# x and the value weights transposed on the host, a second head projected before the first step, a feed-forward loop written out

## The reference

```python
q, k, v = x @ wq, x @ wk, x @ wv              # 8 heads of 128
q, k = rope(q), rope(k)
p = softmax(q @ k.T / 128, causal)
x = layernorm(x + sum over heads of (p @ v) @ wo)
xn, se = rms_norm(x) * gamma_x, rms_norm(slots) * gamma_slot
logits = xn @ se.T                            # 512 slots
slots_in = softmax over the 8 experts (logits).T @ xn
proc = gelu(slots_in @ w1) @ w2
x = layernorm(x + softmax over the 512 slots (logits) @ proc)
```

## Time and profile before

| What | us |
|---|---|
| median of 3 runs | 1684.44 |
| lowest, highest | 1684.43, 1685.83 |
| the profiled execution's own time | 1682.29 |
| its span, first to last instruction | 1680.5 |

### The profile page before, as it was taken

How to read it: one execution, slowest core, us unless ns; L and a number is a source line. 1 busy time by engine, 2 the same in 40 slices (tenths; PEclk the granted TensorE clock), 3 DMA queues, 4 the chain that set the end, 5 groups by cost and what they waited for, 6 DMA issues and landing times. The chain is left out here.

```text
span 1680.5 us, 30759 instructions
## 1 busy us (share of the span) xinstructions
PE 1636.0 (97%) x10524; PEld 1478.8 (88%) x10524; DVE 1223.0 (73%) x2897; ACT 1214.1 (72%) x2425; POOL 1404.5 (84%) x796
## 2 busy tenths in 40 slices
PE   5999999999999999999999999999999997999997
PEld 4899998999899989998999899989999986999997
DVE  5777777777777777777777777777777777677775
ACT  3777777777777777777777777777777764665664
POOL 2889988998899989998999899989988975777784
PEclk9999999999999999999999999999999999999999
DMA  5222232223222322232223222322232323223212
GB/s 150 74 67 77 75 101 67 75 75 100 68 75 75 100 75 76 76 101 77 76 76 101 76 76 76 102 76 76 76 89 76 89 76 97 49 64 97 65 31 57
DMA packets 76489, 133.96 MB, mean 80 GB/s; under 512 B 19264, under 2 KB 45888, under 8 KB 76352
## 3 DMA queue, kind: packets, MB, share of 16 engines
q1 hardware_dynamic: 74880, 130.10, 28.8%
q10 hardware_dynamic: 1472, 2.10, 0.4%
HBM read 56.36 MB, written 8.70 MB: 39 GB/s over the span
## 5 line engine op out<-in xcount | busy, mean ns | idle before, releaser
L633 DVE CUSTOM_DVE_ANT_0 ps_slot<-ps_slot,causal 128x640 f32<-128x640 f32 (+7 forms) x512 | 382.9, 769 | 162.5 <-PE ps_slot L57 162.2
L507 ACT ACTIVATE probs<-ps_slot,neg_max 128x640 f32<-128x640 f32 (+7 forms) x512 | 381.1, 746 | 151.8 <-DVE neg_max L633 151.8
L871 PE MATMUL ps_turn<-ident,probs 128*128 128x128 f32 x2048 | 279.1, 274 | 3.5 <-DVE pt_high L660 2.4
L55 PE MATMUL ps_slot<-k,q 128*128 128x512 f32 (+4 forms) x768 | 273.8, 356 | 3.0 <-ACT probs L507 1.1
L57 PE MATMUL ps_slot<-k,q 128*128 128x512 f32 (+4 forms) x768 | 263.8, 343 | 0.0
L56 PE MATMUL ps_slot<-k,q 128*128 128x512 f32 (+4 forms) x768 | 261.9, 341 | 0.0
L871 PEld LDWEIGHTS ps_turn<-ident,probs 128*128 128x128 f32 x2048 | 232.8, 140 | 23.0 <-issue 3.3
L660 DVE TENSOR_TENSOR pt_split<-ps_turn,pt_split 128x512 fp32r<-128x512 f32 x256 | 175.1, 684 | 93.4 <-ACT pt_split L552 93.4
L442 POOL TENSOR_TENSOR q<-rot_q,q 128x1024 fp32r<-128x1024 f32 x63 | 152.3, 2417 | 63.7 <-ACT q L535 63.7
L426 POOL TENSOR_TENSOR swapped_k<-swapped_k,rope 128x1024 f32<-128x1024 f32 x63 | 151.4, 2404 | 43.7 <-DMA swapped_k<-unrot_k 43.6
L420 POOL TENSOR_TENSOR rot_k<-unrot_k,rope 128x1024 f32<-128x1024 f32 x64 | 154.7, 2417 | 31.2 <-ACT unrot_k L517 31.0
(11 more groups left out here) (188 smaller groups left out, 4428.4 us busy)
## 6 DMA issues: line engine op xcount, KB each, us to landing
swapped_k<-unrot_k SPq DMA_DIRECT2D x128, 256.0 KB, 3.6
swapped_q<-unrot_q SPq DMA_DIRECT2D x128, 256.0 KB, 3.6
inv_b<-inv_rows SPq DMA_DIRECT2D x64, 512.0 KB, 4.7
x_rows<-in_L_attn_x SPq DMA_DIRECT2D x8, 512.0 KB, 5.9
y_t<-y_sum SPq DMA_DIRECT2D x8, 512.0 KB, 5.4
x_rows<-y_t SPq DMA_DIRECT2D x8, 512.0 KB, 3.7
unrot_q<-in_L_attn_x SPq DMA_DIRECT2D x8, 512.0 KB, 5.1
row_b<-r_rows SPq DMA_DIRECT2D x16, 256.0 KB, 3.5
```

Source lines behind the costliest of these rows:

```text
L55: pe.matmul(out, stat_hi, mov_hi, start=start, stop=False, skip_group_check=True)
L507: act.activation(probs_tile(t), score_tile(name, head, i), ACT.Exp, scale=-1.0, bias=neg_max[:, head.par, t:t + 1], accum_out=sums[:, head ...
L633: dve.tensor_tensor_reduce(tile, tile, causal[:, T - WIDTH[t]:T], -1.0, UNSEEN, ALU.add, ALU.min, neg_max[:, head.par, t:t + 1]).then_inc( ...
L871: last = pe.transpose(bank[:, at:at + P], probs_tile(t)[:, j * P:(j + 1) * P], ident[:, :])
```

## The change

x is passed in a second, transposed copy (x_cols: per batch 128 rows of 1024 tokens), and wv comes as (d, h, m) instead of (m, h, d). PE's transposes of x and wv are gone, and ACT and DVE split x out of SBUF, the first half in head 2 and the second in head 3; PE's wait for them moves to head 4. At the start x comes in two halves, wk and wq first for two heads only and later for the other six, whose high parts ACT makes and whose low parts DVE makes. The sine of q of head 0 goes from DVE to POOL. Head 1's k and q are projected before the first values, both pairs of first values go to the banks of ps_turn and ps_y, and step 0 leaves these parts out. The feed-forward loops become Python loops, waits get constants, and wait_apart is gone.

```diff
-                wait_apart(pool, raw_made[1], head.made(), pool_ticks)
+                pool.wait_ge(raw_made[1], head.made())
...
-        self.x_rows = s.sb("x_rows", [P, NT, P], F32)
+        self.x_raw = s.sb("x_raw", [P, T], F32)
...
+FIRST_HEADS = 2
...
-        def loads_x(head):
+        def loads_x(head, half=0):
-            return head.no == X_STEP and head.live() and (not isinstance(head.loop, int) or head.batch() + 1 < B)
+            return head.no == X_STEP + half and head.live() and head.batch() + 1 < B
...
-                sp.dma_start(kept.x_rows[:, :, :], x[batch, :, :].rearrange("(t p) m -> p t m", p=P))\
-                  .then_inc(x_rows_landed, 16)
+                sp.dma_start(kept.x_raw[:, :], x_cols[batch, :, :]).then_inc(x_landed, 16)
...
-            sp.dma_start(kept.x_rows[:, :, :], x[0, :, :].rearrange("(t p) m -> p t m", p=P)).then_inc(first_x_landed, 16)
-            sp.wait_ge(first_x_landed, 16)
+            for half in range(2):
+                sp.dma_start(kept.x_raw[:, half_cols(half)], x_cols[0, :, half_cols(half)])\
+                  .then_inc(first_x_landed[half], 16)
+            sp.wait_ge(first_x_landed[1], 16)
...
-            pool.wait_ge(rope_landed, 32)
+            pool.wait_ge(rope_landed[0], 16)
             mul_cos_k(first)
+            pool.wait_ge(rope_landed[1], 16)
+            mul_sin(0, first)
...
             for n, w in (("k", wk), ("q", wq)):
-                act.dma_start(w_raw[n], w.rearrange("m h d -> m (h d)")).then_inc(w_landed[n], 16)
-            act.wait_ge(first_x_landed, 16)
-            act.dma_start(w_raw["v"], wv.rearrange("m h d -> m (h d)")).then_inc(w_landed["v"], 16)
+                act.dma_start(w_raw[n][:, 0:FIRST_HEADS * D], w[:, 0:FIRST_HEADS, :].rearrange("m h d -> m (h d)"))\
+                   .then_inc(w_landed[n], 16)
+            act.wait_ge(first_x_landed[1], 16)
+            act.dma_start(w_raw["v"], wv.rearrange("d h m -> d (h m)")).then_inc(w_landed["v"], 16)
             act.dma_start(w_raw["o"].rearrange("p (h m) -> p h m", h=H), wo.rearrange("h d m -> d h m"))\
                .then_inc(w_landed["o"], 16)
-            act.wait_ge(first_x_turned, 1)
-            act.activation(kept.x_t[0][:, 0, :], both_y, ACT.Copy).then_inc(first_x_hi, 1)
+            for n, w in (("k", wk), ("q", wq)):
+                act.dma_start(w_raw[n][:, FIRST_HEADS * D:], w[:, FIRST_HEADS:H, :].rearrange("m h d -> m (h d)"))\
+                   .then_inc(rest_landed, 16)
+            for half in range(2):
+                act.wait_ge(first_x_landed[half], 16)
+                act.activation(kept.x_t[0][:, 0, half_cols(half)], kept.x_raw[:, half_cols(half)], ACT.Copy)\
+                   .then_inc(first_x_hi, 1)
             raw_k(first)
             raw_q(first)
-            act.wait_ge(wv_turned, 1)
-            act.activation(wv_t, both_turn, ACT.Copy).then_inc(wv_copied, 1)
             act.wait_ge(wvo_made, 1)
             act.activation(wvo_part(0), both_y, ACT.Copy).then_inc(wvo_hi, 1)
             split_hi(1, first)
+            raw_k(second)
             split_v_hi(first.step(-2))
+            split_hi(0, first)
             split_v_hi(first.step(-1))
+            raw_q(second)
+            split_rest_hi("k", WK_HI, 1.0)
+            split_rest_hi("q", WQ_HI, 1.0 / P)
...
-                split_hi(0, head)
+                if not is_step(head, 0):
+                    split_hi(0, head)
...
-            split_w("k", WK_HI, WK_LO, 1.0)
-            dve.wait_ge(first_x_hi, 1)
-            dve.tensor_tensor(kept.x_t[0][:, 1, :], both_y, f32(kept.x_t[0][:, 0, :]), ALU.subtract).then_inc(first_x_lo, 1)
-            split_w("q", WQ_HI, WQ_LO, 1.0 / P)
+            split_first_w("k", WK_HI, WK_LO, 1.0)
+            split_first_w("q", WQ_HI, WQ_LO, 1.0 / P)
+            for half in range(2):
+                dve.wait_ge(first_x_hi, half + 1)
+                dve.tensor_tensor(kept.x_t[0][:, 1, half_cols(half)], kept.x_raw[:, half_cols(half)],
+                                  f32(kept.x_t[0][:, 0, half_cols(half)]), ALU.subtract).then_inc(first_x_lo, 1)
             mul_cos_q(first)
-            first_rotation(1)
+            first_sin_k()
+            first_add(1)
             dve.wait_ge(wvo_hi, 1)
             dve.tensor_tensor(wvo_part(1), both_y, f32(wvo_part(0)), ALU.subtract).then_inc(wvo_lo, 1)
-            first_rotation(0)
+            first_add(0)
+            first_split_lo(1)
             split_v_lo(first.step(-2))
+            first_split_lo(0)
             split_v_lo(first.step(-1))
-            first_split_lo(1)
-            first_split_lo(0)
+            mul_cos_q(second)
+            split_rest_lo("k", WK_HI, WK_LO, 1.0)
+            split_rest_lo("q", WQ_HI, WQ_LO, 1.0 / P)
...
+                if is_step(head, 1):
+                    pe.wait_ge(w_lo["k"], 2)
+                    pe.wait_ge(w_lo["q"], 2)
+                if loads_x(head.step(-2)):
+                    pe.wait_ge(x_lo, head.batch() * 2 + 2)
-                project_k(after)
+                if not is_step(head, 0):
+                    project_k(after)
...
                 scores("s6", head)
-                if loads_x(head):
-                    for half in range(2):
-                        turn_x(head, half)
                 weigh_split(before)
-                if loads_x(head):
-                    pe.wait_ge(x_lo, head.batch() * 2 + 2)
...
-            for t in range(NT):
-                last = pe.transpose(both_y[:, t * P:(t + 1) * P], kept.x_rows[:, t, :], ident[:, :])
...
             project_q(first, 0)
-            for h in range(H):
-                last = pe.transpose(both_turn[:, h * P:(h + 1) * P], w_raw["v"][:, h * P:(h + 1) * P], ident[:, :])
-            pe.wait_ge(wv_copied, 1)
...
-                last = pe.matmul(both_y[:, own], wv_t[:, own], w_raw["o"][:, own], start=True, stop=True)
+                last = pe.matmul(both_y[:, own], w_raw["v"][:, own], w_raw["o"][:, own], start=True, stop=True)
+            pe.wait_ge(cos_made[0], 2)
+            pe.wait_ge(raw_made[0], 2)
+            project_k(second)
+            pe.wait_ge(raw_made[1], 1)
+            project_q(second, 1)
+            project_q(second, 0)
             pe.wait_ge(wvo_lo, 1)
             project_v(first.step(-2))
+            project_v(first.step(-1))
...
-            with pe.Fori(0, B // 2 - 1) as pair:
+            for pair in range(B // 2 - 1):
                 batch(pair * 2 + 1, 1, False, True)
                 batch(pair * 2 + 2, 0, False, True)
```

More of the change, by code:

```diff
@@ L377, in step @@
                 if loads_x(head.step(2)):
-                    load_x_rows(head.step(2).batch() + 1)
+                    load_x(head.step(2).batch() + 1)
                 spread_inv(before)
@@ L710, in step @@
                 before, after = head.step(-1), head.step(1)
-                mul_cos_q(after)
+                if not is_step(head, 0):
+                    mul_cos_q(after)
                 invert(before)
@@ L732, in step @@
                 rowmax("s6", head)
-                if loads_x(head):
-                    for half in range(2):
+                for half in range(2):
+                    if loads_x(head, half):
                         split_x_lo(head, half)
@@ L889, in turn_shared @@
                 last.then_inc(turned, 1)
-            def turn_x(head, half):
-                pe.wait_ge(x_rows_landed, head.batch() * 16 + 16)
-                pe.wait_ge(turn_lo, head.turns("4b") if half == 1 and "4b" in TURN_AT else
-                           head.step(-1).turns(("3", "10")[half]))
-                for t in range(4 * half, 4 * half + 4):
-                    last = pe.transpose(x_bank(head, half)[:, t % 4 * P:(t % 4 + 1) * P], kept.x_rows[:, t, :],
-                                        ident[:, :])
-                last.then_inc(x_turned, 1)
             def weigh(head, out, probs_t, j_first, start, stop, js=range(4)):
@@ L1008, in step @@
                 turn("6a", head, ("7b", head))
-            pe.wait_ge(consts, 5)
-            pe.wait_ge(first_x_landed, 16)
-            for t in range(NT):
-                last = pe.transpose(both_y[:, t * P:(t + 1) * P], kept.x_rows[:, t, :], ident[:, :])
-            last.then_inc(first_x_turned, 1)
-            first = Head(0, 0, heads)
-            pe.wait_ge(first_x_lo, 1)
+            first, second = Head(0, 0, heads), Head(0, 1, heads)
             pe.wait_ge(w_lo["k"], 1)
-            project_k(first)
+            for half in range(2):
+                pe.wait_ge(first_x_lo, half + 1)
+                last = project_half(1, first, half)
+            last.then_inc(filled["k"], 1)
             pe.wait_ge(w_lo["q"], 1)
@@ L1184, in _ @@
             batch(1, 1, False, False, True)
-            with sp.Fori(1, B // 2 - 1) as pair:
+            for pair in range(1, B // 2 - 1):
                 batch(pair * 2, 0, False, True, True)
@@ L1340, in _ @@
             batch(0, 0, True, True)
-            with act.Fori(0, B // 2 - 1) as pair:
```

(3 more changed lines are left out.)

186 lines of the change are left out of this document (98 added, 88 removed).

## The result

The changed kernel took 1672.8 us (median of four runs, 1672.46 to 1674.66), against 1684.43 us for the kernel before on the same chip: ratio 0.9928, 95% interval 0.9916 to 0.9941, 11.6 us less. The forecast was 1669.6 us with a range of 1664.5 to 1674.5. The profiled execution took 1672.75 us, with a span of 1670.7.

A forecast was written before the change was run, and what follows sets the result against it. TensorE's instruction stream was taken to bound the heads and feed-forward, chains on other engines the start; 8.8 (heads) + 5.4 (start) + 0.6 (feed-forward) = 14.8 us off 1684.44 gives 1669.6 us, range 1664.5 to 1674.5.

The forecast's parts named there:

- Part 1: Heads: removing TensorE's transposes of x saves 1.26 us in each of seven batches, 8.8 us.
- This costs nothing: Heads: ACT and DVE split x out of SBUF within their 5 us of slack per step, at no cost.
- Parts 2 and 3: Start through step 0: first pt_high matmul at 45.7 instead of 51.12 us, 5.4 us gained, bounds 2.9 and 7.6.
- issues four loads of up to 0.47 us (to 6.7): Start, ACT's queue: after x at 4.8 us, four load issues end at 6.7, before the table load and x's copies.
- rows of 1024 take 1.2 us: Start, DVE's queue: each 1024-wide operation ahead of the first row maximum was priced at 1.2 us.
- 2 x 0.95: Start, DVE's queue: the low parts of six heads' wk and wq, 768 wide, at 0.95 us each, ending at 31.7.
- Part 3: Step 0 after the first row maximum: ACT's wait for POOL's rotated k of head 1 goes, 1.5 us more gained.
- I let them end before: Start: the other loads, 2.75 MB instead of 2.0, start 3 us earlier and were assumed not to delay k's swap.
- Part 4: Feed-forward written out: 0.1 us gained for each of six batches, 0.6 us; bounds nothing and 2.5 us.
- case D: Feed-forward written out gains nothing, the rest as forecast: 1670.2 us; chance 0.66 shared with the main forecast.
- C: Feed-forward slower: written-out code needs 12 instruction packets, each stopping TensorE 2.4 us, 28.8 us in all; 1699.0 us, chance 0.03.
- A: Start gives only 1 to 2 us because a late wait shifts DVE's queue; 1673.5 us, chance 0.14.

The follow-up runs named there:

- experiment 2: Kernel before, with only x's columns loaded and split out of SBUF for the batches after the first; 1673.97 us, ratio 0.9948.
- experiment 1: Changed kernel with the feed-forward hardware loops and register waits of before; 1671.7 us, ratio 0.9928.
- Experiment 4: Separate small kernel, not the layer: DVE operations alone or beside POOL products; two-SBUF-input subtraction 512 wide 0.69 us alone, 2.71 beside POOL.
- 7: Changed kernel with the six other heads' wk and wq low parts made inside step 0, wk's behind the first row maximum, plus filler matmuls; 1671.21 us.
- 10: Changed kernel with early table load, late low parts, fillers, 28 transposes before the first k matmul, rest's loads behind wvo's high-part copy; 1665.34 us, ratio 0.9889.
- experiment 5: Changed kernel with ACT's table loaded early by a dummy activation and loads of the rest of wk and wq behind x's copies; 1670.25 us, ratio 0.9918.
- experiment 9: Changed kernel with early table load and loads of the rest of wk and wq behind ACT's copy of wvo's high parts; 1666.22 us, ratio 0.9901.
- 6: Changed kernel with filler matmuls, results unread, in TensorE's waits of the start; 1671.67 us, ratio 0.9925.
- 3: Changed kernel with low parts of the six other heads' wk and wq made inside step 0, without fillers; 1674.03 us, ratio 0.9941.
- 8: Changed kernel with early table load, loads behind x's copies, late low parts, fillers and 40 transposes before the first k matmul; 1668.4 us, ratio 0.9904.

## Why the prediction was right, and where a step was wrong

**Part 1, the heads:** right, 8.97 us for the 8.8 forecast, and experiment 2 gives the same alone. "This costs nothing" held, with a wrong price: each half's subtraction took 2.2 us, not 0.69, since it now reads SBUF only and waits for POOL. DVE's slack covered it. The bound given for the case without that cover, 1.5 us a batch, was too low: two such subtractions more than fill it.

**Parts 2 and 3, the start:** this term was mis-sized, 1.4 us instead of 5.4 and below its bound of 2.9; the profiled execution of experiment 1, with the same start, had 0.4. The forecast by stations:

| | before | forecast | after |
|---|---|---|---|
| first k matmul | 12.31 | 9.3 | 11.13 |
| sine product of k on DVE | 20.62 | 17.6 | 19.54 |
| first row maximum | 35.58 | 31.7 | 36.51 |
| first pt_high matmul | 51.12 | 45.7 | 49.74 |

Two steps failed. First, "issues four loads of up to 0.47 us (to 6.7)": x came at 5.3 instead of 4.8, and the issues took 0.36, 0.46, 0.60 and 1.45 us, until 8.3. Of the 1.8 us by which the k matmul was later than forecast, 0.5 is x, 1.1 the issues and 0.2 the way from the table load to the matmul. Second, the durations on DVE's queue, "rows of 1024 take 1.2 us" and "2 x 0.95" for the rest's low parts. They were read beside an idle POOL. The forecast itself let POOL start on head 1 ten us earlier, and so put POOL's products beside them: low q took 2.46 instead of 1.22 us, and the two low parts 3.31 instead of 1.9. From the sine product to the row maximum it was 2.9 us more than forecast: 1.2 for low q, 1.4 for the two low parts, 0.5 by which POOL's sine of q was late, and 0.8 in which DVE waited for ACT's high parts of the rest, a wait that the forecast did not have; less 0.7 for the cosine products of q, between which no copy of ACT stood, and 0.3 because operations followed each other a little faster than at 1.2 us. Experiment 4 shows the mechanism by itself, 7 and 10 that less backlog brings the row maximum forward.

Part 3's wait went as forecast and gave more: from row maximum to pt_high matmul 13.2 instead of 15.5 us, 14.0 in experiment 1 with the low clock throughout. "I let them end before", of the heavier loads, held in the kernel after, where the swap took as long as before; once k came earlier it did not (5 against 9).

The clock: a stretch at 1.2 GHz fell on the first scores, behind TensorE's wait of 5.05 us, and cost nothing one can see; the stretch behind the first row maximum cost some tenths of a us here and more in experiments 1 and 5 (6). The Trainium skill's rule in "TensorE: Matmul & The Clock Gate", section "HAM oscillation — how this bites in real kernels", which the prediction cited, had that stretch there. That it moves the executions by some 2 us in the feed-forward's first batch was not in the forecast.

**Part 4:** 0.6 us forecast, nothing found (1): case D of the rivals. C fell with it: more packets were fetched and no batch was longer.

**The rivals.** A comes nearest to what happened, 1.5 us in the start and 1673.5 in all, and one of its reasons (four issues ahead of ACT's first copy) was the right one; the other half, DVE beside POOL, no case had. The time was in the range because the largest term was exact and the range reached as far as A. Some luck is in it: the two profiled spans lie 9.8 us apart, which from the median before gives 1674.6, just outside, and the 1.8 us more between the medians are in no trace. Two slips changed nothing: the bound of 1673.3 comes out as 1672.7 from its own terms (8.8 + 2.9 + 0), and A's "nine operations" ahead of the first row maximum are twelve by part 2's own list.

## What to carry to other kernels

Before a backlog on VectorE is costed, look at what GpSimd does beside it in the new order: here operations whose inputs were all in SBUF took 2.0 us longer beside it, so a duration read beside an idle GpSimd is too short. When data is brought in earlier, walk its first consumer's own queue, load issues and table load included, and put loads that are needed last behind the small transfers on the path. A gain at one station counts only at the next one where engines meet: here 3.4 us at the first matmul were 1.0 at the first row maximum until two loads were moved. And before a small difference at a station is put down to an edit, compare the granted clock behind it: the same start came out 1.0 us apart in two executions.

## What the runs showed of the hardware that was not expected

- Beside GpSimd's products a subtraction of 128 x 512 out of two SBUF tensors took 2.71 us instead of 0.69, one of 128 x 1024 3.25 instead of 1.23, a multiplication of one SBUF tensor 2.45 instead of 0.43; out of PSUM it stayed at 0.69.
- The last of four load issues in a row on ScalarE took 1.45 us, the first 0.36. Whether the queue or its descriptors hold it was not tried.
- A swap of two times 256 KB, used 4.4 us after its issue in the kernel after, was used 6.9 us after it behind loads that were still running (experiment 5), and 4.4 us after it once two of these were moved (experiment 9).
- Where a stretch at 1.2 GHz falls depends on the execution and on edits far away: in the four kernels with the low parts late (3, 7, 8, 10) one fell into the heads' last steps, between 1353 and 1371 us, and the heads took 1.6 us longer; in the profiled executions of the others it did not. Whether the shift in time or the other order does it was not tried.
